# A new order of ScalarE and VectorE work in the opening of a fused FFN and convolution kernel

## What is computed

```python
def dequant_nf4(q, absmax, shape):
    w = NF4_CODE[q.reshape(-1)]
    w = w.reshape(-1, BLOCK) * absmax[:, None]
    return w.reshape(shape)
...
Wg = dequant_nf4(gate_q, gate_absmax, (M, HD))     # M = 1792, HD = 512
Wu = dequant_nf4(up_q, up_absmax, (M, HD))
Wd = dequant_nf4(down_q, down_absmax, (HD, M))
g = jnp.einsum('bsh,mh->bsm', x, Wg)
u = jnp.einsum('bsh,mh->bsm', x, Wu)
h = jax.nn.silu(g) * u
return jnp.einsum('bsm,hm->bsh', h, Wd)
...
x = L0_attn_u
xn = _layernorm(x, axis=-1)
x = x + _L0_attn_ref(xn, ...) + _L0_ffn_ref(xn, ...)
```

## Time and profile before

| what | value |
|---|---|
| time, median of 3 runs | 504.59 us (504.0 to 504.82) |
| the profiled execution | 504.82 us |
| its span, first to last instruction | 502.9 us |
| PE busy | 475.6 us (95%) |
| DVE busy | 294.6 us (59%) |
| ACT busy | 210.6 us (42%) |
| TensorE clock granted, mean | 0.993 of full |

### The profile page before, as it was taken

The page is one execution under the profiler, slowest core; times in us unless marked ns, Lnnn a source line. Parts: engine busy times, 40 slices in busy tenths (PEclk is TensorE's granted clock), DMA queues, the critical chain, the costliest instruction groups (busy, mean ns, idle before and its releaser), DMA issues.

```text
span 502.9 us, 6080 instructions
## 1 busy us (share of the span) xinstructions
PE 475.6 (95%) x2283; PEld 224.8 (45%) x2283; DVE 294.6 (59%) x565; ACT 210.6 (42%) x369; POOL 13.2 (3%) x46
## 2 busy tenths in 40 slices
PE   0469999999999999999999999999999999999997
PEld 0334444444444444444444454466444444444443
DVE  4999867666565666776577757765677613000013
ACT  4467765455445554455444525578563000000000
POOL 0000071000000000000000000000000000000000
PEclk9988999999999999999999999999999999999999
DMA  7854662121111121111211112234331702200013
GB/s 253 251 126 111 121 189 63 43 63 54 52 44 44 60 65 42 43 56 50 63 44 42 46 39 53 73 85 150 103 101 47 237 15 94 74 0 1 0 42 126
DMA packets 32828, 39.76 MB, mean 79 GB/s; under 512 B 16224, under 2 KB 16544, under 8 KB 32800
## 3 DMA queue, kind: packets, MB, share of 16 engines
q1 hardware_dynamic: 32800, 39.38, 26.7%
HBM read 32.03 MB, written 4.19 MB: 72 GB/s over the span
## 4 chain that ended last, share of the span: by engine, by line
PE 93%; DVE 3%; DMA 2%; ACT 1%; SPq 1%; issue 0%; DVEq 0%
PE bank L1013 57%; PE bank L1112 29%; PE bank L1102 5%; DMA qs<-in_q_up 1%; PE bank L1035 1%; PE bank L1075 1%; DMA xT<-h 1%; DVE h L647 1%; ACT h L420 0%; ACT h L455 0%; DVE h L691 0%; ACT h L467 0%; SPq L276 0%; DVE h L572 0%; DVE wt L572 0%
## 5 line engine op out<-in xcount | busy, mean ns | idle before, releaser
L1013 PE MATMUL bank<-xT,w 128*128 128x512 f16 x1344 | 293.7, 382 | 4.3 <-DMA xT<-h 3.3
L1013 PEld LDWEIGHTS bank<-xT,w 128*128 128x128 f16 x1344 | 132.0, 98 | 164.5 <-issue 3.8
L1112 PE MATMUL bank<-wd,h 128*128 128x512 f16 x672 | 145.2, 379 | 0.0
L420 ACT ACTIVATE knee<-qs 128x512 f32<-128x512 int32 x164 | 98.0, 621 | 8.1 <-DMA qs<-in_q_gate 6.6
L1112 PEld LDWEIGHTS bank<-wd,h 128*128 128x128 f16 (+1 forms) x672 | 65.7, 98 | 79.1
L593 DVE SCALAR_TENSOR_TENSOR bank<-bank,sc,sil 128x512 f32<-128x512 f32 x56 | 42.5, 759 | 70.6 <-PE bank L1013 64.1
L448 ACT ACTIVATE h<-bank 128x512 f16<-128x512 f32 x56 | 33.4, 597 | 73.0 <-DVE bank L593 73.0
L999 DVE SCALAR_TENSOR_TENSOR xT<-bank,sc,xT 128x512 f32<-128x512 f32 x16 | 11.4, 748 | 84.3 <-PE bank L1112 84.3
L442 ACT ACTIVATE sil<-bank,sc 128x512 f32<-128x512 f32 x56 | 38.0, 679 | 18.3 <-PE bank L1013 18.2
L598 DVE TENSOR_TENSOR h<-bank,h 128x512 bf16<-128x512 f32 x56 | 38.6, 690 | 10.5 <-ACT h L448 9.2
L559 DVE SCALAR_TENSOR_TENSOR acc_r<-knee 128x512 f32<-128x512 f32 x41 | 28.1, 685 | 20.2 <-ACT knee L420 20.2
(11 more groups left out here) (93 smaller groups left out, 125.1 us busy)
## 6 DMA issues: line engine op xcount, KB each, us to landing
h<-in_x SPq DMA_DIRECT2D x8, 512.0 KB, 9.2
w<-in_x SPq DMA_DIRECT2D x16, 256.0 KB, 3.5
out<-xT SPq DMA_DIRECT2D x16, 256.0 KB, 2.0
qs<-in_q_gate SPq DMA_DIRECT2D x14, 256.0 KB, 2.7
qs<-in_q_up SPq DMA_DIRECT2D x14, 256.0 KB, 2.6
am<-in_am_gate SPq DMA_DIRECT2D x28, 128.0 KB, 2.9
am<-in_am_up SPq DMA_DIRECT2D x28, 128.0 KB, 2.9
qs<-in_q_down SPq DMA_DIRECT2D x14, 256.0 KB, 2.7
```

Source lines behind the costliest of these rows:

```text
L420: nc.scalar.activation(knee_of(u, k), qs[:, u % 2, :], KNEE, scale=scale, bias=bias, alpha=below).then_inc(knee_done, 1)
L1013: mm = nc.tensor.matmul(out_b[:], w1[:, k % 2, unit, wl, f, :], xT[:, TPC * c:TPC * c + TPC, xl, f, :], start=(i == 0), stop=(i == 3 * NC ...
L1112: mm = nc.tensor.matmul(bank[(t + 4) % 8][:], part, wd[:, mt, wl, :], start=(mt == 0 and n == 0), stop=(mt == NM - 1 and n == 2))
```

## The change

It rewrites a piece of the hand-written order on ACT and on DVE. The set of operations is the same on every engine. PE's and SP's orders are as before.

```diff
@@ ACT
             h_hi(1)
             silu(2)
+            items(25, 27)
             norm(12)
             norm(13)
             x_hi(12)
+            h_hi(2)
             norm(14)
             x_hi(13)
             norm(15)
             x_hi(14)
-            h_hi(2)
             x_hi(15)
             silu(3)
-            items(25, 27)
+            items(28, 30)
             h_hi(3)
-            items(28, 30)
             silu(4)
@@ DVE
             h_mul(0)
-            stats(12)
             weight_lo(3)
-            stats(13)
             x_lo(8)
-            stats(14)
+            items(24, 25)
             x_lo(9)
-            stats(15)
+            items(25, 26)
+            x_lo(10)
+            h_lo(0)
+            x_lo(11)
+            h_mul(1)
+            for t in range(12, 16):
+                stats(t)
             moments(12, 16)
-            x_lo(10)
-            rstd(2, 0)
-            rstd(2, 1)
-            h_lo(0)
-            rstd(2, 2)
-            rstd(2, 3)
-            x_lo(11)
-            for i in range(4, 7):
+            for i in range(4):
                 rstd(2, i)
-            h_mul(1)
-            for i in range(7, RSTD):
+            items(27, 28)
+            rstd(2, 4)
+            rstd(2, 5)
+            h_lo(1)
+            rstd(2, 6)
+            rstd(2, 7)
+            items(28, 29)
+            rstd(2, 8)
+            rstd(2, 9)
+            items(29, 30)
+            for i in range(10, RSTD):
                 rstd(2, i)
-            items(24, 25)
-            h_lo(1)
-            items(25, 26)
+            h_mul(2)
             x_lo(12)
-            h_mul(2)
+            h_lo(2)
             x_lo(13)
+            h_mul(3)
             x_lo(14)
-            h_lo(2)
             x_lo(15)
-            items(27, 30)
-            h_mul(3)
             h_lo(3)
             items(30, 32)
             h_mul(4)
```

## The result

| | before | changed |
|---|---|---|
| median | 504.29 us (503.98 to 504.82, 4 runs) | 510.72 us (510.23 to 511.73, 4 runs) |
| profiled execution | 504.82 us | 511.18 us |
| its span | 502.9 us | 509.2 us |

The ratio of the changed kernel to the one before is 1.0129, with a 95% interval of 1.011 to 1.0147: the change costs 6.4 us. The forecast was 511.5 us.

A forecast was written before the change was run, and what follows sets the result against it. PE alone was taken to bound the kernel after 36.16 us. A 4.1 us stall before round 6 (a round is 24 matmuls) plus 2.8 us of clock loss, added to the 504.59 us median, gave 511.5 us, range 508.6 to 513.2.

The forecast's parts named there:

- The bound: After 36.16 us nothing but PE sets the end; the edits come later, so there is nothing to win.
- Step 1, statistics: On DVE, the rstd chain of tiles 12 to 15 ends at 56.9 us, 4.3 us later than now.
- Step 2, ACT: On ACT, norm(12) waits for the rstd chain until 56.9 us; silu(3) runs from 62.3 to 63.0.
- Step 3, `h_mul(3)`: On DVE, h_mul(3) ahead of x_lo(14) and x_lo(15) waits for silu(3); x_lo(15) ends at 65.0 us, now 59.05.
- Step 4, the transposes: On SyncE's queue, last transpose issued at 65.8 us; PE starts round 6 at 69.0 instead of 64.9, stalling 4.1 us.
- Step 4, the codes of weight 6: On SyncE's queue, their load moves from 63.84 to about 70.2 us; weight 5 keeps 1.0 us margin; costed at nothing.
- rival B: Second PE stall at round 8, codes of weight 6 and weight 5 late, 1 to 2 us: 512.5 to 513.5; 7%.
- Step 5, the clock: On PE, behind the 4.1 us gap, half clock for 14 matmuls costs 2.8 us more than full clock.
- A: At round 6, PE stalls without losing clock: 508.7 us; 7%.
- C: At round 6, chunk 3 still arrives in time, so not slower: 504.6 us; 6%.
- D: On PE behind 42 us, the earlier work on weight 4 makes the kernel faster, no size given; 1%.
- E: At round 6, only half the delay holds because silu(3) comes early, stall 2.2 us: 506.8 to 509.6; 4%.

The follow-up runs named there:

- `tail_undone`: Changed kernel with h_mul(3) moved back behind x_lo(15) on VectorE: 508.76 us.
- `stats_undone`: Changed kernel with stats, moments and rstd of tiles 12 to 15 put back among the x_lo, h_mul(3) still ahead of x_lo(14): 506.95 us.
- `both_undone`: Changed kernel with both h_mul(3) and the statistics of tiles 12 to 15 put back, the rest of the change kept: 505.31 us.
- `wide_fill_codes_first`: Changed kernel with 17 extra 512-column matmuls ahead of round 6 and the codes of weights 6 and 7 issued before the table loads: 508.86 us.
- `before_wide_fill`: Kernel before with 14 extra 512-column matmuls between rounds 0 and 1 and the codes of weights 6 and 7 issued before the table loads: 503.86 us.
- `fill_gap`: Changed kernel with 34 extra 256-column matmuls on TensorE ahead of round 6, while it waits for chunk 3: 510.77 us.
- `after_codes_first`: Changed kernel with only the codes of weights 6 and 7 issued ahead of the table loads on SyncE's queue: 510.56 us.
- `scalar_part_alone`: Kernel before with the changed order on ScalarE only, VectorE's order as before: 507.68 us.
- `fill_gap_codes_first`: Changed kernel with 34 extra 256-column matmuls ahead of round 6 and the codes of weights 6 and 7 issued before the table loads: 511.47 us.
- `before_filled`: Kernel before with 28 extra 256-column matmuls on TensorE between rounds 0 and 1: 504.19 us.

## Why the prediction was right, point by point

- **The bound.** PE alone sets the end from the start of round 6; with the constant taken from the kernel before, the ledger closes within 0.1 us in the changed kernel, `tail_undone`, `stats_undone`, `both_undone`, `wide_fill_codes_first` and `before_wide_fill` (63.9 + 438.0 = 501.9, its span). But "nothing to win" rested on one execution. Where PE comes through the opening faster, its inputs bind: `before_wide_fill` is that case.
- **Step 1, statistics.** Last `rstd` step forecast to end at 56.9, measured 56.48. `h_mul(0)` itself was 0.35 us earlier in that execution (42.49), which is nearly the whole difference. Undoing it wins 3.8 us (510.72 to 506.95), but in the profiles only 1.4 us of that is an earlier round 6; the rest is the clock loss, which is gone. What the prediction says of the two knees of weight 5, that they cost nothing, holds only because the statistics are later still.
- **Step 2, ACT.** `silu(3)` from 62.3 forecast, 61.90 measured; the same 0.4 us.
- **Step 3, `h_mul(3)`.** `x_lo(15)` forecast to end at 65.0, measured 63.35 + 1.28 = 64.63. Undoing it wins 2.0 us (510.72 to 508.76), 1.45 us of it by the start of round 6.
- **Step 4, the transposes.** Last issue forecast 65.8, measured 65.3; round 6 forecast 69.0, measured 68.62. The stall was mis-sized as a gap: 4.1 us forecast, 5.1 measured, because PE arrived 1.4 us earlier than in the profile of before. The end does not see that, since it goes by when chunk 3 lands. The prediction gives both, the gap and the start time; the start time is what counts. The shift of that start, 4.1 forecast, was 3.7.
- **Step 4, the codes of weight 6, costed at nothing.** True for the changed kernel: they were issued at 69.72, `weight_lo(5)` ended at 83.15, and PE wanted it at 68.62 + 2.6 + 60 x 0.216 = 84.2, the margin of 1.0 us that the prediction names. In `fill_gap`, at full clock and with the codes 2.5 us later, they cost 1.34 us. So rival B's mechanism exists; that the slow clock hid it in the changed kernel is not shown.
- **Step 5, the clock.** 2.8 us forecast from one row, 2.6 in the profile after, 1.7 as the difference of two timed kernels. The Trainium skill ("TensorE: Matmul & The Clock Gate", "What's actually happening") says of the start of a kernel that the number of slow matmuls varies from run to run. Behind gaps in the middle of this kernel it varies too: behind the late start of round 6 it was 13 in the changed kernel and 8 in `tail_undone`, and in round 1 it was 14 before and 8 in the changed kernel. In `after_codes_first` the ledger leaves only 507.9 - 68.62 - 438.0 = 1.3 us for the clock, with the same start of round 6 as in the changed kernel. That 2.8 came so close to the profile's 2.6 is therefore partly luck: it was the only row I had, and other gaps in these runs cost anything from 0 to 2.8 us. The range of this term, 1.6 to 3.6 us, is not worked out in the prediction, and no trace read here shows more than 14 slow matmuls. For the profiled execution the forecast was 511.7 against 511.18, of which 0.4 is the start of round 6 and 0.2 the clock. The median lies a further 0.3 us lower than I set it; no trace says why.
- **The rivals.** A (no clock loss, 508.7), C and D did not happen. E is what `tail_undone` makes, 508.76, inside its 506.8 to 509.6.

## What to carry to other kernels

In a hand-written order, give each input of the bound engine a deadline and its margin; an operation moved earlier is paid for by everything it overtakes, here a chain of tiny dependent steps that a whole chunk of tokens waits for. Before an operation that waits for another engine is placed ahead of ready work on an in-order queue, look whether that other engine has yet to pass the same ready work. Forecast a stall by when the late input arrives, not by the length of the gap. And read an undone part by its trace: with one cause removed, the next operation in the queue, here two knees, held the same input.

## What the runs showed of the hardware

- **The length of a gap on TensorE did not tell what it cost in clock.** In front of round 1 a gap of 3.2 to 3.3 us cost 14 slow matmuls before, 8 in the changed kernel and none in `after_codes_first`. In front of round 6 gaps of 5.1 and 5.2 us cost 2.6 us (changed) and 1.3 us (`after_codes_first`, an estimate by the ledger), one of 3.3 us cost 1.7 (`tail_undone`), and one of only 2.47 us cost clock as well (`scalar_part_alone`), while one of 1.78 us cost none (`stats_undone`). Windows of PE (busy, count, clock, DMA share, GB/s), two from `after_codes_first`, behind its first gap and behind its second, then one from `scalar_part_alone`:

```profile
35.80:43.00 7.20, 7.20 (x34) 1.00 0.33 102
68.70:71.20 2.50, 2.50 (x7) 0.50 0.68 242
...
66.58:70.20 3.62, 3.62 (x10) 0.54 0.78 251
```

- **A fetch of instructions seems to slow the transfers in flight.** In `fill_gap_codes_first` two transposes landed 4.4 to 4.8 us after issue around such a packet, in `before_filled` one after 4.9 us; elsewhere they take 3.0 to 3.9. Halving the number of fill instructions removed both delays. That the packet is the cause was not isolated: the width of the fill changed with it. Nor does every such packet delay a transpose: in `fill_gap` one stands between 68.3 and 68.6 us, and the last transpose, still in flight, landed after no more than 3.3 us.
- **Two losses at one place need not add.** In the kernel before, a late weight and a late chunk take up what a full clock gives (`before_wide_fill`); in `stats_undone` two knees take up a part of what the earlier statistics give.
